# Where a tile's transpose and low-rank product stand among the eight chunks of the next tile

## The reference

```
h      = x[s] @ A[ids[s]].T          # 16 columns: the adapter's rank
out[s] = x[s] + x[s] @ W.T + bias + h @ B[ids[s]].T
```

## Time and profile before

| | us |
|---|---|
| median of 3 runs | 1334.47 (1333.99 to 1334.64) |
| the profiled execution | 1329.43 |
| its span, first to last instruction | 1327.7 |
| PE busy in the span | 1314.6 (99%) |
| PE's weight loads busy | 1207.3 (91%) |
| DVE busy | 625.5 (47%) |
| ACT busy | 223.3 (17%) |
| POOL busy | 203.0 (15%) |

### The profile page before, as it was taken

One profiled execution on the slowest core, in us unless ns is written; L12 is line 12 of the kernel. 1 busy time (PEld: TensorE's weight loads), 2 busy tenths in 40 slices (PEclk: granted clock), 3 DMA queues, 4 the chain that ended last, 5 costly groups with the idle time before them and its releaser, 6 DMA issues.

```text
span 1327.7 us, 18317 instructions
## 1 busy us (share of the span) xinstructions
PE 1314.6 (99%) x7160; PEld 1207.3 (91%) x7160; DVE 625.5 (47%) x832; ACT 223.3 (17%) x408; POOL 203.0 (15%) x98
## 2 busy tenths in 40 slices
PE   9999999999999999999999999999999999999998
PEld 9999999999997888899999999999888888888887
DVE  4334435645445444556556844345534444533322
ACT  4111212111221000221101211112211111211110
POOL 0000012322210000035454421232000000000000
PEclk9999999999999999999999999999999999999999
DMA  5577777887577777776767845764666788855552
GB/s 201 191 246 243 251 265 259 280 293 246 193 280 262 255 242 232 244 263 243 243 235 274 305 135 167 232 212 158 207 236 240 238 269 297 291 187 192 196 192 108
DMA packets 93658, 308.80 MB, mean 233 GB/s; under 512 B 10498, under 2 KB 19762, under 8 KB 93618
## 3 DMA queue, kind: packets, MB, share of 16 engines
q1 hardware_dynamic: 93618, 308.35, 68.5%
HBM read 211.82 MB, written 97.01 MB: 233 GB/s over the span
## 4 chain that ended last, share of the span: by engine, by line
PE 87%; DMA 5%; SPq 3%; DVE 3%; POOL 1%; issue 1%; ACT 0%; DVEq 0%; ACTq 0%; POOLq 0%
PE acc L944 30%; PE acc L956 28%; PE acc L949 26%; DMA pool<-wT 3%; PE acc L990 2%; SPq L315 1%; DMA pool<-x 1%; SPq L403 1%; POOL pool L878 1%; DMA w_raw<-w_sums 1%; SPq L334 1%; DVE h_cols L768 0%; DMA pool<-xT 0%; SPq L504 0%; SPq L474 0%
## 5 line engine op out<-in xcount | busy, mean ns | idle before, releaser
L956 PE MATMUL acc<-w_lo,x_hi 128*128 128x320 f32 (+2 forms) x2302 | 563.5, 344 | 1.7 <-DVE w_lo L708 1.7
L956 PEld LDWEIGHTS acc<-w_lo,x_hi 128*128 128x128 f32 x2302 | 399.7, 188 | 35.2 <-DVE w_lo L708 2.0
L944 PE MATMUL acc<-w_hi,x_hi 128*128 128x352 f32 x1536 | 334.5, 326 | 0.8 <-ACT w_hi L602 0.8
L944 PE MATMUL acc<-w_hi,x_lo 128*128 128x352 f32 (+1 forms) x1536 | 329.2, 322 | 0.0
L944 PEld LDWEIGHTS acc<-w_hi,x_lo 128*128 128x128 f32 x1536 | 262.3, 189 | 0.0
L944 PEld LDWEIGHTS acc<-w_hi,x_hi 128*128 128x128 f32 x1536 | 258.6, 189 | 1.1 <-DVE w_hi L716 1.0
L949 PE MATMUL acc<-w_hi,x_hi 128*128 128x512 f32 x766 | 241.4, 396 | 0.1
L949 PE MATMUL acc<-w_hi,x_lo 128*128 128x512 f32 x766 | 238.9, 392 | 0.0
L597 ACT ACTIVATE x_hi<-pool 128x1024 fp32r<-128x1024 f32 x110 | 116.2, 1057 | 717.2 <-PE acc L956 361.9
L893 POOL TENSOR_TENSOR pool<-pool,keep 128x1024 f32<-128x1024 f32 x48 | 130.5, 2734 | 409.5 <-DMA pool<-x 409.5
L703 DVE TENSOR_TENSOR x_lo<-pool,x_hi 128x1024 fp32r<-128x1024 f32 x110 | 167.3, 1521 | 49.8 <-ACT x_hi L597 49.8
(11 more groups left out here) (44 smaller groups left out, 410.8 us busy)
## 6 DMA issues: line engine op xcount, KB each, us to landing
pool<-xT SPq DMA_DIRECT2D x142, 512.0 KB, 5.8
pool<-x SPq DMA_DIRECT2D x64, 512.0 KB, 5.6
out<-pool SPq DMA_DIRECT2D x47, 512.0 KB, 2.8
pool<-wT SPq DMA_DIRECT2D x32, 512.0 KB, 7.7
w_sums<-pool SPq DMA_DIRECT2D x32, 512.0 KB, 3.6
w_raw<-w_sums SPq DMA_DIRECT2D x32, 512.0 KB, 6.5
s_sums<-pool SPq DMA_DIRECT2D x32, 512.0 KB, 7.5
pool<-s_sums SPq DMA_DIRECT2D x32, 512.0 KB, 5.3
```

Source lines behind the costliest of these rows:

```text
L944: mm = nc.tensor.matmul(acc[j][:, o, low:high], xs, w_hi[:, s, base + o * COLS_A + low:base + o * COLS_A + high], start=(k == 0 and part = ...
L956: mm = nc.tensor.matmul(acc[j][:, o, low:low + n], x_hi[:, j, k], w_lo[:, slot(ph, k), first:first + n], start=False, stop=end and (ph not ...
```

## The change

Two constants change. The turn of h stands behind the third chunk of the next tile in place of the second, and the low-rank product behind the fifth in place of the third. Between them there are two chunks in place of one. No instruction is added or removed; `LAST_TURN` and `LAST_LORA` stay.

```diff
-TURN_AFTER, LORA_AFTER = 1, 2
+TURN_AFTER, LORA_AFTER = 2, 4
```

## The result

The changed kernel takes 1327.00 us (median of five runs, 1326.24 to 1328.46), against 1333.99 us for five runs of the kernel before in the same comparison: a ratio on record of 0.9956 [0.9939, 0.9973] (the quotient of the two medians is 0.9948).

What follows compares the result with a forecast made beforehand. PE was taken as the bound, with 6.26 us of stops removable. Gains of 4.79 less losses of 2.2 and 0.2 gave -2.4, from a median of 1334.47 to 1332.1 us, range 1328.5 to 1335.0.

Steps and rivals of the forecast that it cites:

- The bound and the ceiling: PE is busy 1314.6 of 1327.7 us; its six stops at the two moved steps, 6.26 us, are the most removable.
- P2's tile 2: Stop at the low-rank product, `h_stack` late behind x's rounding on ACT; two chunks cover it, a gain of 0.44 us.
- P4's last tile: Stop at the low-rank product, `h_stack` late behind x's rounding on ACT; two chunks cover it, a gain of 1.51 us.
- P2's tile 7: Turn's stop of 1.10 us, `h_cols` ending with POOL's second addition; gain 0 to 1.10 by POOL's slide, taken 0.45.
- P2's tile 10: Turn's stop of 1.98 us, `h_cols` late beside POOL; gain 1.43 to 1.98, taken 1.70.
- P6's tile 0: Passage from P2: later `read_out` closes DVE's hole for POOL's addition, P6's tile 1 starts 2.2 us later; 0.54 stop no gain.
- The end: Last tile's unmoved turn waits for `h_cols`, made behind the later `read_out`: loss of 0 to 0.3 us, taken 0.2.
- The slack in P7 and P3: x's low part stands behind `read_out`; its slack of 4.39 us ahead of the tile becomes 1.61 and costs nothing.
- 5.04: Microseconds by which the runs' median lay above the profiled execution; carried over unchanged, turning 1334.47 - 2.4 into 1332.1.
- No collision at P6: Rival, 28%: POOL's addition finds a gap and the gains stand, 1329.9 us, or 1329.1 with P2's two stops wholly gone.
- New stops in P2 in place of the old: Rival, 13%: POOL's pair meets the h sums at the moved place, both turn stops return; 1334.2 us.
- the late accumulator: Rival, 7%, slower: in P7 and P3 the accumulator is read too late, 1351 us, or about 1341 in every second tile.

Runs made afterwards that it cites:

- experiment 4: The kernel before, unchanged, timed in twelve runs (median 1329.18 us, ratio 1.0006) and profiled in further executions; the eight profiles have a mean of 1330.5 us.
- experiment 5: One comparison against the kernel before (1332.42 us): changed kernel 1327.39; turn and low-rank product one chunk later each 1325.60; later still in P2 and P4 1325.04.
- copy 2: A further profiled execution of the unchanged kernel before: 1327.93 us, with 3.38 us of stops at the two moved steps.
- copies 5 and 7: Two further profiled executions of the unchanged kernel before: 1332.53 and 1333.90 us, with 8.02 and 6.98 us of stops at the two moved steps.
- copies 6 and 7: Two further profiled executions of the unchanged kernel before: 1331.47 and 1333.90 us; their P2 tile 0 took 16.24 and 15.43 us.
- the earlier trace: The profiled execution of the unchanged kernel before that was shown ahead of the prediction: 1329.43 us, with 6.26 us of stops at the two moved steps.
- copy 7: A further profiled execution of the unchanged kernel before: 1333.90 us, 6.98 us of stops at the two moved steps, granted clock 0.997.

## Why the prediction was wrong

**The bound and the ceiling: right.** PE is busy 99% after as before, and what moved is its stops.

**Gains, forecast 4.79 us.** By the lengths of the tiles they are 5.05. P2's tile 2: 12.46 to 12.04, 0.42 (0.44). P4's last tile: 13.52 to 12.04, 1.48 (1.51). P4's tile 5: 12.71 to 12.04, 0.67 (0.69). P2's tile 7: 13.13 to 12.04, 1.09, where 0.45 was taken between 0 and 1.10: POOL slid 1.5 us against the tile (its addition starts 0.54 us behind the tile's start, before 0.97 ahead of it), and with that the low part of h had to wait for one addition and not for two. The text names this case, "beyond about 1.4 `h_cols` slips in ahead of it", and then takes another s. P2's tile 10: 14.01 to 12.62, 1.39 (1.70): there POOL kept its place and one chunk is what it covered.

**Losses, forecast 2.4 us.** P6's tile 0 grows from 12.29 to 14.08, 1.79, where 2.2 was taken; the mechanism is the one described, row by row, POOL's addition behind x's split and the weight split standing for it. The end costs a stop of 0.44 at the turn, but by the length of the last tile 0.27 (16.52 to 16.79) against 0.2. One sign was missed: P6's tile 1 waits 1.85 us and not 2 or more, as tile 0 pays a part ahead of it, 0.94 for 0.54 at the turn and 0.21 at a weight split. The slack in P7 and P3 costs nothing, as forecast; the Trainium skill's rule (Perfetto Trace Analysis, Optimization Strategy), by which a gap that repeats can mean too little PSUM for the next tile, found no such gap here.

**The sum: right within a microsecond.** -5.05 + 1.79 + 0.27 is -3.0; the profiled executions differ by 3.19, forecast 2.4. The other 0.2 lie in the first tiles of P1 and P2, which the change does not touch.

**The step that failed** is the sentence "The median of the runs is 5.04 us above that execution; I carry the 5.04 over as it is". After the change the five runs' median is 1327.00 - 1326.24 = 0.76 above the profiled execution. 5.04 - 0.76 = 4.28 of the 5.1 us of error are this step, 0.8 the sum. The 5.04 was no cost around the profile: the kernel before takes 1326 to 1337 us, and three runs had come from the upper part, while the profile lies below the middle (the median of the 79 runs below is 1330.55). All of its runs in three comparisons and its twelve of experiment 4, with all of the changed kernel's, by the granted clock of the whole execution (of the first comparison the record gives the clock for the changed kernel alone):

| granted clock | before: runs, mean us | changed: runs, mean us |
|---|---|---|
| 1.000 | 30, 1328.93 | 12, 1327.03 |
| 0.999 | 24, 1330.82 | 3, 1327.94 |
| 0.998 | 11, 1333.19 | 2, 1328.66 |
| 0.996 to 0.997 | 14, 1334.32 | none |
| all | 79, 1331.05 | 17, 1327.38 |

At full clock the change is worth 1.90 us, near the -2.4 of the forecast; over all executions 3.67. (In the one comparison of experiment 5 alone it is 1.43 at full clock and 4.21 over all.) The rest goes with executions of a lower granted clock, 49 of 79 before and 5 of 17 after, and the prediction's sum has no term for it: it took the clock as full from one execution. A row of 0.999 need not hold a fall that costs time, though: copy 2 shows 0.999, and its clock falls only after PE's last matmul. In the profiles of copies 5 and 7 the clock falls behind a stop of over 2 us at the turn, the kind that the change shortens (last section); in copies 6 and 7 it falls in P2's tile 0, behind a stop that either kernel has. How the 1.8 us between 1.90 and 3.67 divide between these and the longer stops themselves is not settled. That the three first runs were of this kind is argued from their times (1333.99 to 1334.64) alone.

**The rivals.** No collision at P6 would have given 1329.9, closer to the time, for a wrong reason: the collision is there. (With P2's two stops wholly gone its sum is 1329.0, not 1329.1.) New stops in P2 in place of the old did not come, nor did the late accumulator.

## What to carry to other kernels

A profile is one execution: where two engines can meet, look at several before the distance between it and the timed runs is taken for a constant, and give the range the spread of the kernel before. Slack of one chunk ahead of a wait can be worth more in other executions than in the one that was profiled: a stop of 2.50 us would give back 1.43, one of 0.40 no more than 0.40. A step that is moved later for the sake of its producer also releases its consumers later, so move it by no more than the wait needs: here one chunk for the turn was the whole gain, and the low-rank product's second chunk only cost.

## What the runs showed of the hardware

**DVE beside POOL.** With POOL's additions cut, DVE's rows sum to 532.5 us in place of 625.5: 93 us of what the page calls busy is DVE standing beside POOL, while the kernel gains 10 us (1331.75 to 1321.51). An instruction of 16 columns takes 0.17 us alone and up to 2.4 beside POOL's addition, by how much of that is still to run. The Trainium skill (SBUF — State Buffer, Who interferes with whom) says that of a DVE instruction with two inputs in SBUF and a GpSimd instruction that reads SBUF, the second to issue is held until the first is done. The trace agrees. A DVE instruction with one input in PSUM is not held: beside the first addition of the earlier trace rows the first h sum takes its usual 0.19 us, while the second, with both inputs in SBUF, takes 1.03 behind it; and in the whole execution 58 pieces of `read_out` (L803) that start inside an addition take about 0.5 us each, as outside. In the timeline of DVE, kernel before:

```profile
280.15 0.19 DVE L759 TENSOR_TENSOR h_sum<-acc,h_part 128x32 f32<-128x32 f32 x1 [5.81 <-PE acc L956]
280.38 1.03 DVE L762 TENSOR_TENSOR h_keep<-h_sum 128x16 f32<-128x16 f32 x1
```

One thing more: POOL came in between two DVE instructions that were queued back to back (385.82 and 386.68 above), so whole queues of DVE shift by one POOL addition.

**The clock.** In copy 7 PE's granted clock falls to half twice before its last matmul, each time behind a stop; in the execution of the earlier trace rows it does not. The windows (stretch, length, busy us of PE, PEld, DVE, ACT, POOL with instructions, granted clock, DMA share, GB/s), copy 7 first, then the kernel before:

```profile
206.50:209.50 3.00, 3.00 (x13) 3.00 (x12) 0.64 (x2) 0.00 (x0) 0.00 (x0) 0.50 0.85 294
250.70:253.70 3.00, 3.00 (x12) 3.00 (x13) 1.10 (x3) 0.28 (x1) 0.00 (x0) 0.52 0.85 254
```

```profile
206.50:209.50 3.00, 3.00 (x20) 3.00 (x20) 0.76 (x4) 1.54 (x4) 0.00 (x0) 1.00 0.82 283
```

Weight loads of copy 7: the ends of the two stops, and the turn behind the first; then the same two steps of the kernel before:

```profile
205.95 0.45 PEld L956 LDWEIGHTS acc<-w_lo,x_hi 128*128 128x128 f32 x3 [2.04 <-DVE w_lo L708]
...
212.22 0.19 PEld L979 LDWEIGHTS turned<-eye,h_cols 128*128 128x128 f32 x1
...
250.52 0.18 PEld L979 LDWEIGHTS turned<-eye,h_cols 128*128 128x128 f32 x1 [2.16 <-issue]
```

```profile
205.28 0.44 PEld L956 LDWEIGHTS acc<-w_lo,x_hi 128*128 128x128 f32 x3 [2.04 <-DVE w_lo L708]
...
210.00 0.19 PEld L979 LDWEIGHTS turned<-eye,h_cols 128*128 128x128 f32 x1
```

At 1.2 GHz (0.50) 13 matmuls of PE lie in 3 us, at 2.4 GHz (1.00) 20, both times without a gap. From the end of the stop to the turn copy 7 takes 212.22 - 205.95 = 6.27 us, the execution before 4.72: one fall costs 1.55 us, beside the stop itself. All profiles together show seven such falls in P2, each at a stop of 2.02 to 2.54 us (six behind it, one 0.27 us before its end), and eight stops of 2.00 to 2.50 us, the one at 205.28 among them, with none. What decides between the two is not shown. In the two profiles of the changed kernel the stops at the moved steps are at most 0.94 us, and behind none of them did the clock fall.
